# Clearing four scatter accumulators: from SyncE's program of the norm stage to ACT's queue in the set-up, in 36 transfers for 200

## What is computed

```python
xn = _layernorm(x)                                  # 12500 x 256
x = x + gnn(xn, src, dst, edge_weight, ...) + mix(xn[None], ...)[0]
x = x + ffn(_layernorm(x)[None], ...)[0]

def gnn(x, edge_row, edge_col, edge_val, weight_l, bias_l, weight_r, bias_r):
    h = x @ weight_l
    msgs = edge_val[:, None] * h[edge_col]
    agg = jax.ops.segment_sum(msgs, edge_row, num_segments=N)
    return agg + bias_l + x @ weight_r + bias_r
```

## Time and profile before

| what | us |
|---|---|
| median of 3 runs | 5057.96 |
| lowest, highest | 5052.91, 5059.99 |
| the profiled execution | 5066.14 |
| its span | 5064.2 |
| PE busy | 3791.3 (75%) |
| POOL busy | 3300.9 (65%) |
| DVE busy | 2295.8 (45%) |
| ACT busy | 1245.6 (25%) |

### The profile page before, as it was taken

The page is one execution under the profiler, slowest core; times in us unless marked ns, Lnnn a source line. Parts: engine busy times, 40 slices in busy tenths (PEclk is TensorE's granted clock), DMA queues, the critical chain, the costliest instruction groups (busy, mean ns, idle before and its releaser), DMA issues. The chain is left out here.

```text
span 5064.2 us, 84566 instructions
## 1 busy us (share of the span) xinstructions
PE 3791.3 (75%) x16502; PEld 2994.5 (59%) x16634; DVE 2295.8 (45%) x10289; ACT 1245.6 (25%) x2628; POOL 3300.9 (65%) x2297
## 2 busy tenths in 40 slices
PE   4777777777777777777777777764888849999995
PEld 3555555555555555555555555542555528888885
DVE  4444444444444445555555555542656641222221
ACT  1222222222222222222222222221011003444442
POOL 1336888888888888888888888885444423444442
PEclk9998888888888888888888888876555559999998
DMA  6996777777777777777777777767656655666666
GB/s 196 340 319 92 97 98 98 96 99 96 98 95 99 96 100 104 105 105 109 104 105 106 108 104 105 107 81 159 207 194 199 198 146 135 142 145 145 142 142 182
DMA packets 644846, 683.19 MB, mean 135 GB/s; under 512 B 65384, under 2 KB 599364, under 8 KB 644546
## 3 DMA queue, kind: packets, MB, share of 16 engines
q0 software_dynamic: 293040, 312.13, 46.2%
q1 hardware_dynamic: 338178, 361.33, 23.5%
q10 hardware_dynamic: 13584, 9.24, 0.7%
HBM read 280.99 MB, written 414.27 MB: 137 GB/s over the span
## 5 line engine op out<-in xcount | busy, mean ns | idle before, releaser
L818 POOL DMA_INDIRECT agg<-msg,sidx x1664 | 2580.4, 1551 | 541.0 <-issue 376.7
L1016 PE MATMUL bank<-rows,Cmat 128*128 (+1 forms) x3328 | 1032.5, 448 | 167.1 <-ACT msg L1166 164.4
L1166 ACT COPY msg<-bank 128x512 f32<-128x512 f32 x832 | 487.0, 585 | 2250.4 <-DMA agg<-msg,sidx 1963.0
L1016 PEld LDWEIGHTS bank<-rows,Cmat 128*128 128x128 f32 x3328 | 686.1, 223 | 391.3 <-issue 303.5
L883 DVE SCALAR_TENSOR_TENSOR sidx<-seen_sum,trash,srcf 128x4 int32<-128x4 f32 x416 | 92.6, 223 | 1458.6 <-DMA agg<-msg,sidx 1458.4
L1895 POOL DMA_INDIRECT x_rows_and_trash<-x_y,x_node x224 | 345.1, 1541 | 547.5 <-DVE x_y L1879 497.8
L1001 PE MATMUL bank<-Emat,pick 128*128 128x128 f32 x3328 | 545.2, 317 | 195.1 <-DVE seen L870 192.4
L866 DVE TENSOR_SCALAR Emat<-bank,srcf,wtf 128x128 f32<-128x128 f32 x1664 | 565.0, 399 | 0.0
L1001 PEld LDWEIGHTS bank<-Emat,pick 128*128 128x128 f32 x3328 | 516.9, 229 | 51.3 <-issue 17.0
L870 DVE SCALAR_TENSOR_TENSOR seen<-bank,srcf,prior 128x128 f32<-128x128 f32 x1664 | 479.7, 342 | 0.0
L1808 PE MATMUL bank<-x_xf,x_w 128*128 128x256 f32 x1792 | 407.5, 381 | 1.3 <-ACT x_xf L1836 1.3
(11 more groups left out here) (243 smaller groups left out, 4153.4 us busy)
## 6 DMA issues: line engine op xcount, KB each, us to landing
x_w<-in_L_ffn_W_dram SPq DMA_DIRECT2D x112, 512.0 KB, 4.9
agg<-zeros SPq DMA_DIRECT2D x196, 256.0 KB, 5.1
r_agg<-agg SPq DMA_DIRECT2D x196, 256.0 KB, 4.4
x_zin<-expert_table SPq DMA_DIRECT2D x112, 259.0 KB, 5.1
rows<-h_rows SPq DMA_DIRECT2D x208, 128.0 KB, 2.8
agg<-msg,sidx POOLq DMA_INDIRECT x1664, 3.8
xn_rows<-xnr POOLq DMA_DIRECT2D x49, 256.0 KB, 4.7
xn_turned<-xnT POOLq DMA_DIRECT2D x49, 256.0 KB, 4.9
```

The source lines that it names most:

```text
L818: pool.indirect_dma_start(scratch["agg"][r][:, :], bass.IndirectOffsetOnAxis(ap=sidx[:, j:j + 1], axis=0), msg[:, j % (2 * BATCH), :], Non ...
L1016: mm = nc.tensor.matmul(M[p][:, (q % 2) * D:(q % 2 + 1) * D], Cmat[:, b % 2, q, :], rows[:, bass.ds(slot, 1), :], start=True, stop=True)
L1166: nc.scalar.copy(msg[:, at:at + 2, :].rearrange("p q c -> p (q c)"), M[p][:, :]).then_inc(s_msg, 1)
```

## The change

The clears leave SP's norm program. ACT gets a program in the set-up: it waits until the loads of the edge lists and of `wide` have landed, then issues 9 x 4 transfers, each of 11 x 128 = 1408 rows (1.44 MB) of one accumulator. Partition p of `zeros` gives 11 consecutive rows, read from the same 256 elements 11 times. The semaphore that counts them moves to the outer level, since SP still waits for it at the end of the norm phase. The bytes cleared are the same, 51.9 MB.

```diff
+CLEAR_ROWS = 11
+CLEARS = AGG_ROWS // P // CLEAR_ROWS
+assert CLEARS * CLEAR_ROWS * P == AGG_ROWS
...
+        s_zeroed = sem("accumulators_cleared")
...
             sp.wait_ge(s_plan, 64)
+
+        @block.scalar
+        def _(act):
+
+            act.wait_ge(s_load, 16 * 11)
+            act.wait_ge(s_wide, 96)
+            for n in range(CLEARS):
+                for acc in scratch["agg"]:
+                    act.dma_start(acc[n * CLEAR_ROWS * P:(n + 1) * CLEAR_ROWS * P, :].rearrange("(p a) d -> p a d", p=P),
+                                  zeros[:, 0:D].rearrange("p (a d) -> p a d", a=1).to_broadcast([P, CLEAR_ROWS, D])
+                                  ).then_inc(s_zeroed, 16)
...
-            def clear(i, tiles=2):
-
-                for acc in scratch["agg"]:
-                    sp.dma_start(acc[bass.ds(i * 2 * P, tiles * P), :].rearrange("(a p) d -> p a d", p=P),
-                                 zeros[:, 0:tiles * D].rearrange("p (a d) -> p a d", a=tiles)).then_inc(s_zeroed, 16)
-
-            def body(k, u):
-                load(k, u)
-                clear(2 * k + u)
-
-            over_pairs(sp, body)
-            clear(PAIRS, tiles=(AGG_ROWS - NPAD) // P)
-            sp.wait_ge(s_zeroed, 16 * NACC * (PAIRS + 1))
+            over_pairs(sp, load)
+            sp.wait_ge(s_zeroed, 16 * NACC * CLEARS)
```

More of the change, by code:

```diff
@@ L102, in build @@
                      base=base_row, general=general)
+        s_zeroed = sem("accumulators_cleared")
         setup_phase(nc, ctx, t, scratch, psum, ident, prior, trash, fill_at, iota8, ones, zeros,
-                    lower, iotaq, nodes, base, run, edges)
+                    lower, iotaq, nodes, base, run, edges, s_zeroed)
         with ExitStack() as mid:
@@ L107, in build @@
             wk = mid.enter_context(nc.sbuf_tensor("wk", [P, HALF, D], F32))
-            norm_phase(nc, t, scratch, psum, ident, zeros, gscale, kmax, wk)
+            norm_phase(nc, t, scratch, psum, ident, s_zeroed, gscale, kmax, wk)
             edge_mix_phase(nc, t, scratch, psum, ident, prior, trash, ones, zeros, gscale,
@@ L118, in setup_phase @@
 def setup_phase(nc, outer, t, scratch, psum, ident, prior, trash, fill_at, iota8, ones, zeros,
-                lower, iotaq, nodes, base, run, edges):
+                lower, iotaq, nodes, base, run, edges, s_zeroed):
     with ExitStack() as ctx:
@@ L335, in first, with norm_phase @@
     return isinstance(i, int) and i == 0
-def norm_phase(nc, t, scratch, psum, ident, zeros, gscale, kmax, wk):
+def norm_phase(nc, t, scratch, psum, ident, s_zeroed, gscale, kmax, wk):
     with ExitStack() as ctx:
@@ L376, in norm_phase @@
         s_fin = sem("n_gate_variance")
-        s_zeroed = sem("n_accumulators_cleared")
         s_gstd = sem("n_gate_std")
```

## The result

The changed kernel takes 5073.14 us (median of 7 runs, 5070.64 to 5076.18), the kernel before 5057.96 (7 runs, 5052.44 to 5060.96). The ratio is 1.0032, with a 95% interval of 1.0021 to 1.0044: slower by 15 us. I had forecast 5062 with a range of 5010 to 5083; the time lies in the range, and 11 us over the forecast.

The account below looks back on a forecast made before the run. DMA was taken to bound the norm stage, with PE next. Barrier at 168.7 plus a norm stage of 216.7 put the edge stage at 385.4, 3.9 us later; against the median of 5057.96 that gave 5062 us, range 5010 to 5083.

Parts of the forecast that it names:

- PE's 3.96 us a pair: Norm stage: with the clears gone, PE sets the pace at 0.50 + 3.46 us a pair, taken as 4.0.
- the drain: Set-up: ACT's clears move at 355 GB/s, 4.06 us a transfer, so the barrier opens at 168.7 us, not 65.7.
- a queue that holds 1.1 to 2.2 MB: ACT's queue in the set-up: stops its engine at that many bytes, so two transfers outstanding after the last issue.
- my other bound: ACT's queue in the set-up: the count of transfers matters, 8 outstanding; ACT free 24 us earlier, 8 given back.
- Rival 1: Set-up: ACT's issues are not held, ACT reaches the barrier at 54 us; 5015 us in all; chance 0.14.
- Rival 2: Set-up: the clears' new form drains at a lower rate, 192 GB/s; +120 us, 5178; chance 0.18.
- the first turn: Norm stage's start: 7.7 us to PE's first turn of a pair, as in the kernel before.
- my 194.0: Norm stage, first turn to last: 48 periods of 4.0 us = 192.0, plus 2 us for first products at half clock.
- my 15.0: Norm stage's end: 15.0 us from the last turn to the edge stage, as in the kernel before.
- 99 us won, 103 lost: Whole change: norm stage 99 us shorter, barrier held 103 us, edge stage 3.9 us later.
- a period of 4.3 us: Norm stage: upper bound for a pair, 3.96 divided by the mean clock of 0.92; +14 us.

Follow-up runs that it names:

- the queue run: Against the kernel before: the 200 clears stay in the norm stage, four after each pair, but ACT issues them in place of SP; 5066.27 us, ratio 1.0017.
- the old form: Against the change: all four accumulators cleared from ACT's queue in the set-up, but in 200 transfers of 256 KB; 5077.77 us, ratio 1.0035 to the kernel before.

## Why the prediction was right, and where it was 11 us off

**Right: what bounds the kernel, and what bounds it next.** I said that bytes set the norm stage's pace and that PE's 3.96 us a pair would be next. The pairs take 3.92, the clock is 1.00, DVE's waits for x are 11.9 us in place of 135.6, and the queue run shows that the waits for x were waits for bandwidth.

**Right: ACT is held by the drain, with two transfers left, and the barrier with it.** The issues take 4.12 us, and by 173.5 at 343 GB/s 34 transfers were done. But that it was two came in part by luck. I had worked it out from a queue that holds 1.1 to 2.2 MB; 3.02 MB were left, and the old form on the same queue leaves 0.67. So it was not a limit in bytes that held ACT here. The count was nearly the same with both sizes, 2.1 and 2.5, and far from the 8 of my other bound. Rival 1, which had the issues cheap, falls: the first two took 0.67 and 0.96 us, like the single large one, and from the third on they did not (3.59, then 4.1). One issue with nothing queued around it says nothing of 36 in a row. Rival 2, a slow drain of the new form, falls too: 343 GB/s, for the old form in the same place 340.

**Off by 5.4 us: the drain, above all its rate.** I took 355 GB/s from two stretches at 338 and 368; it was 343. That is 4.8 us over 34 transfers, and most of the rest of the barrier's 5.4 (174.1 for 168.7) is the start: data moved from 30.8 us, where I had 30.1. The window at 368 was 8 us long; the 220 us at 338 were the better guide.

**Off by 4.8 us: the first turn.** "7.7 us from its start to the first turn as now" was wrong: it took 12.5 (174.20 to 186.66), because the two transfers that I had left outstanding stood ahead of the first x. I had given such a price only to the bound with 8 of them. The old form with 0.26 MB left had 7.6.

**The rest cancels.** From the first turn to the last 192.3 us for my 194.0; from the last turn to the edge stage 16.7 for my 15.0: the last pair's load came late, PE idled 2.55 us before the last turn, and the products behind it began at the lower clock (1.91 us for 1.03). That these two cancel is luck. 3.9 + 5.4 + 4.8 - 1.7 + 1.7 = 14.1, the 14.2 measured. "99 us won, 103 lost" was 94 won, 108 lost.

So the mechanism was right, and two terms of the sum were too small: the rate, and what the leftover transfers cost behind the barrier. As the two large terms nearly cancel, 5% of either is 5 us, a third of the effect, and I could not tell the sign with confidence: I gave slower by over 0.2% a chance of 0.37. That is what came, and not the 0.45 for within 0.2% that I thought likeliest; the time lies near the range's upper end, and most of the width there came from a period of 4.3 us that did not occur. What I did not see before the runs is the more useful thing: the gain and the loss do not grow together. A quarter of the change is a gain of 35 us, half of it one of 39.

Not tried: the same transfers from a queue whose issues do not hold their engine. POOL comes to the set-up's barrier at 3.5 us, and the issues of its stores took 0.73 us each before the change and after it. That would separate what the held barrier costs from what the bytes cost.

## What to carry to other kernels

Moving work of a saturated resource into an idle stretch pays for as much as the stretch can hold, here about one accumulator of four (36.9 us won for 0.2). What is moved beyond that holds the barrier about as long as it frees the stage behind it (32.9 against 36.8 us), and it is a plain loss once another engine is the limit there, here somewhere between two and three accumulators. Work out both amounts first. SP and ACT, when they issued more transfers than their queue took, were stopped at the rate of the drain, so ask what stands behind an engine's issues in its own program; a barrier there makes the stop everybody's. And a wait for a load, under saturated DMA, can be a wait for bytes: here changing the queue only moved the wait to another name.

## What the runs showed of the hardware that I had not expected

- The rate of the clears hardly depended on the size of a transfer once the queue was full: 343 GB/s with 1.44 MB each, 340 with 256 KB. In the norm stage, with loads and stores beside the clears, it was 338 GB/s before the change and 352 with two accumulators moved.
- ACT's queue held more bytes when its transfers were larger: when an issue returned, 2.0 to 2.1 transfers of 1.44 MB had not moved (3.0 MB), against 2.5 of 256 KB (0.67 MB). Landing time over issue time, by which I had counted before, gives 3.3 and 4.3: it counts the transfer that is being issued too.
- Beside a queue with large transfers always waiting, the set-up's 17 loads landed at 45.6 us in place of 29.1, though the engines were not full before (share 0.64 from 0 to 29 us). I had expected 8 us.
- POOL's issues of stores did not slow with saturation: 0.73 us each in the norm stage, at a DMA share of 1.03 before and of 0.80 after the change. Only SP's and ACT's did (the median issue of SP's transfers of 256 KB was 1.10 us for the clears before the change, and 0.37 for the loads of x after it).
